# Four engines' order lists redrawn in a four-layer graph kernel

## What is computed

```python
x = layernorm(x + L0(x, adj))   # hypergraph conv, relu, layer norm, hypergraph conv, + x
x = layernorm(x + L1(x, adj))   # w = q . (adj @ k) / 16, softmax over the nodes, times v
x = layernorm(x + L2(x, adj))   # attention of 8 heads, scores * (adj + adj), softmax
x = layernorm(x + L3(x, adj))   # gated attention:
#   gate = sigmoid(deg * Wd + bd); xg = x * gate
#   QK = sigmoid(xg @ Wqk.T + bqk); s = (QK @ QK.T / 16) * adj; attn = s / (sum(s) + 1e-6)
#   out = relu(attn @ xg @ Wl.T + bl + xg @ Wr.T)
```

## Time and profile before

| | |
|---|---|
| median of 3 runs | 1077.64 us (1073.41 to 1079.28) |
| the profiled execution | 1074.29 us, span 1072.5 us |
| TensorE busy | 951.3 us (89%), mean granted clock 0.964 |
| VectorE busy | 881.4 us (82%) |
| GpSimd busy | 737.1 us (69%) |
| ScalarE busy | 711.0 us (66%) |
| HBM | 41 GB/s over the span |

### The profile page before, as it was taken

How to read it: one execution, slowest core, us unless ns; L and a number is a source line. 1 busy time by engine, 2 the same in 40 slices (tenths; PEclk the granted TensorE clock), 3 DMA queues, 4 the chain that set the end, 5 groups by cost and what they waited for, 6 DMA issues and landing times. The chain is left out here.

```text
span 1072.5 us, 32446 instructions
## 1 busy us (share of the span) xinstructions
PE 951.3 (89%) x11228; PEld 818.5 (76%) x11228; DVE 881.4 (82%) x2503; ACT 711.0 (66%) x1516; POOL 737.1 (69%) x1163
## 2 busy tenths in 40 slices
PE   3467789999999999999999999999999999998853
PEld 2346668888888888888888888888888888887642
DVE  4334668999999999999999999999999999988752
ACT  2234557776777777777777777777777777776642
POOL 3244566777778777777777887777777778875442
PEclk9588989999999999999999999999999999999996
DMA  7110222222212222222221222222222212211200
GB/s 203 30 31 2 56 58 59 64 59 64 60 50 53 63 57 66 66 66 62 59 60 52 53 57 66 57 66 66 66 57 61 61 51 53 59 49 46 53 24 20
DMA packets 110231, 61.80 MB, mean 58 GB/s; under 512 B 57072, under 2 KB 105840, under 8 KB 110192
## 3 DMA queue, kind: packets, MB, share of 16 engines
q1 hardware_dynamic: 110192, 61.30, 22.0%
HBM read 35.83 MB, written 8.39 MB: 41 GB/s over the span
## 5 line engine op out<-in xcount | busy, mean ns | idle before, releaser
L1219 POOL TENSOR_TENSOR gp<-late,bdb 128x512 f32<-128x512 f32 x32 | 40.6, 1270 | 98.0 <-ACT late L846 98.0
L460 PE MATMUL bank<-z1h,W 128*128 128x256 f16 x256 | 71.0, 277 | 2.9 <-DVE z1l L898 2.9
L462 PE MATMUL bank<-W,rFl 128*128 128x256 f16 x256 | 72.7, 284 | 0.0
L461 PE MATMUL bank<-W,rFh 128*128 128x256 f16 x256 | 72.7, 284 | 0.0
L460 PE MATMUL bank<-W,rFh 128*128 128x256 f16 x256 | 72.6, 284 | 0.0
L739 ACT ACTIVATE x<-preB,nbB,rsB 128x256 f32<-128x256 f32 x64 | 34.9, 593 | 55.1 <-POOL nbB L1214 55.1
L461 PE MATMUL bank<-z1l,W 128*128 128x256 f16 x256 | 70.7, 276 | 0.0
L462 PE MATMUL bank<-z1h,W 128*128 128x256 f16 x256 | 70.6, 276 | 0.0
L739 ACT ACTIVATE late<-preG,nbG,rsG 128x256 f32<-128x256 f32 x64 | 34.9, 592 | 52.6 <-POOL nbG L1214 52.6
L1289 POOL TENSOR_TENSOR late<-late,Smx 128x512 f32<-128x512 f32 x64 | 66.8, 1043 | 4.2 <-DVE Smx L1109 3.9
L766 ACT ACTIVATE r<-bank,b1c 128x256 f32<-128x256 f32 x128 | 53.4, 469 | 8.3 <-PE bank L462 6.2
(11 more groups left out here) (286 smaller groups left out, 4573.2 us busy)
## 6 DMA issues: line engine op xcount, KB each, us to landing
Vbd<-vst SPq DMA_DIRECT2D x128, 66.0 KB, 2.1
xin<-x SPq DMA_DIRECT2D x32, 256.0 KB, 2.7
xres<-x SPq DMA_DIRECT2D x32, 256.0 KB, 2.8
Kbd<-kst SPq DMA_DIRECT2D x128, 64.0 KB, 2.0
out<-late SPq DMA_DIRECT2D x32, 256.0 KB, 2.2
mrow<-mask SPq DMA_DIRECT2D x32, 128.0 KB, 3.2
atA<-adj_t SPq DMA_DIRECT2D x64, 32.0 KB, 2.3
aC<-adj SPq DMA_DIRECT2D x64, 32.0 KB, 2.1
```

The lines of the kernel that those rows point to most:

```text
L460: pe.matmul(o, sh, mh, start=start, stop=False, skip_group_check=True)
L461: pe.matmul(o, sh, ml, start=False, stop=False, skip_group_check=True)
L462: return pe.matmul(o, sl, mh, start=False, stop=stop, skip_group_check=True)
L1219: return pool.tensor_tensor(dst, src, b[:].rearrange("p (o d) -> p o d", o=1).broadcast_to([P, TILES, D]), ALU.add)
```

## The change

The four lists are replaced. Each has the same entries in another order: the same pieces run, with the same waits.

```diff
-ORDER_PE = [4, 2, 3, 1, 5, 3, 0, 4, 2, 5, 0, 4, 2, 1, 5, 0, 3, 2, 3, 0, 0, 1, 5, 4, 5, 1, 3, 5, 2, 3, 0, 0, 1, 2, 4]
-ORDER_ACT = [3, 0, 5, 1, 3, 5, 0, 2, 5, 0, 4, 4, 0, 4, 5, 1, 0, 3, 0, 1, 0, 0, 0, 0, 2, 4, 3, 1, 2, 5, 4, 3, 2, 4, 5]
-ORDER_DVE = [4, 0, 4, 0, 0, 0, 2, 0, 1, 0, 3, 0, 4, 0, 2, 4, 0, 4, 3, 5, 5, 2, 0, 1, 2, 1, 5, 1, 0, 4, 3, 3, 2, 2, 2, 3, 3, 1, 5, 4, 5, 4, 4, 0, 5, 5, 0, 1, 2, 3, 1, 5, 0, 5, 1, 0, 3, 2, 4]
-ORDER_POOL = [0, 0, 0, 1, 3, 1, 0, 4, 1, 1, 1, 1, 3, 5, 2, 2, 2, 3, 0, 0, 0, 4, 4, 4, 5, 4, 5, 0, 5, 0, 5, 0]
+ORDER_PE = [2, 1, 4, 3, 5, 0, 4, 2, 3, 2, 0, 5, 1, 4, 0, 2, 5, 3, 0, 0, 3, 1, 5, 4, 5, 1, 5, 3, 2, 3, 1, 0, 2, 0, 4]
+ORDER_ACT = [0, 4, 3, 1, 5, 2, 0, 5, 0, 3, 5, 4, 0, 4, 4, 5, 1, 0, 0, 0, 1, 0, 0, 0, 3, 2, 1, 3, 2, 5, 4, 3, 2, 4, 5]
+ORDER_DVE = [0, 0, 4, 0, 0, 2, 0, 2, 0, 1, 0, 4, 0, 4, 0, 4, 3, 5, 4, 0, 2, 2, 1, 5, 1, 3, 1, 0, 2, 5, 2, 3, 2, 4, 3, 3, 3, 1, 5, 0, 4, 5, 4, 5, 4, 1, 5, 2, 3, 1, 5, 5, 0, 1, 0, 3, 2, 4, 0]
+ORDER_POOL = [0, 0, 0, 1, 1, 0, 4, 3, 1, 1, 1, 1, 5, 2, 2, 3, 2, 0, 3, 0, 4, 0, 4, 4, 5, 4, 5, 5, 5, 0, 0, 0]
```

## The result

The changed kernel takes **1032.45 us** (median of 4 runs, 1028.01 to 1033.61), against 1077.59 for the kernel before in the same comparison. The ratio is 0.9579, with a 95% interval of 0.954 to 0.9618. The forecast was 1051 with a range of 1038 to 1068: the sign was right, and the gain of 45 us was under-estimated by 18.6. The executions of one kernel differ, and their mean granted clock with them: the changed kernel's have 0.962 three times and 0.969 in the one of 1028.01.

A forecast was written before the change was run, and what follows sets the result against it. TensorE was taken to set the pace, VectorE close behind. 22.7 us from 27 full steps plus 4 from the first steps made 26.7 off 1074.29, so 1047.6; with 3.35 up to the median, 1051, range 1038 to 1068.

The forecast's parts named there:

- (a): VectorE's HBl pair, moved clear of GpSimd's large instructions, costs 0.66 us instead of 1.94; not counted beyond the waits.
- (b), (c), (d): TensorE's waits for wrm (L598), HBl (M and D) and the row sums of r go, together 1.2 us a step.
- The floor of a full step: TensorE's step of 29.54 us, less 1.2 us of waits that can go, is 28.34 us.
- (e): Chain from sc1 over rFl, preF and xg takes 11.08 us against TensorE's 10.72: a new wait of 0.36 us a step.
- (f): Ql meets xl and pcol meets bias work, pushing preB and z1l about 0.6 us; counted at nothing, up to 0.3 a step.
- (g): In the first steps most of TensorE's waits for HBl go: 4 us won, bounds 1 and 7.
- (h): The last steps, without stream 0, keep layer 3's chain in the same order: no change, 2 us either way.
- A: Rival: nothing new is late and the new wait is hidden; 36.4 us won, 1041 us; chance 0.12.
- B: Rival: the gain comes back as small waits, a step of 29.3 us; 9.5 us won, 1068 us; chance 0.13.
- C: Rival: HBl's second half misses its gap, waits for xres+b2b, 1.15 us late; step 29.85, 1082 us; chance 0.06.
- D: Rival: GpSimd goes first when Ssb ends, rFl stands another 1.28 us; step 29.98, 1085.5 us; chance 0.06.

The follow-up runs named there:

- the undo: The changed kernel with VectorE's rFl put back behind mvF, as in the kernel before; 1021.9 us, ratio 0.9494 to the kernel before.

## Why the prediction was wrong, point by point

- **(a) HBl clear of GpSimd: right.** Predicted 0.66 us for the pair, measured 0.59. The margin was 0.4 us, and more in fact: VectorE and GpSimd in the changed kernel, from rvar on:

```profile
518.43 0.15 DVE L1015 SCALAR_TENSOR_TENSOR rvar<-bank,rmm 128x2 f32<-128x2 f32 x1
...
520.39 0.59 DVE L898 SCALAR_TENSOR_TENSOR HBl<-HT,be,HBh 128x128 f16<-128x128 f16 x2
```

```profile
521.37 1.27 POOL L1219 TENSOR_TENSOR xres<-xres,b2b 128x512 f32<-128x512 f32 x1
```

  HBl ends at 520.98, and xres+b2b starts 2.94 us behind rvar instead of 2.70. The remark that HBl's freedom buys 0.1 us by itself was made for a step that still waits for wrm, and doesn't carry over: the swap with y0 cost 1.4 us in every full step, 1.1 of them a wait of TensorE.
- **(b), (c), (d) The three waits go: right.** The trace after has none of them in full steps.
- **The floor of a full step: the term that failed.** I took 28.34 us, and the run with rFl moved shows 28.01 with no wait left. All gaps over 0.04 us in TensorE's timeline of one step add up to about 2.7 us before and to 1.2 in that run. I had read three of them, 1.41 us, left 0.07 of each for a hand-over and took the rest as fixed: 1.5 us would have stayed. But the gaps ahead of M and D and of the row sums are gone entirely, and so are those of 0.13 us ahead of s3 and of the xg turn, which the idle times don't count as waits. That is 0.33 us a step, 8.9 us in all.
- **(e) The new wait: right in what causes it and in size.** rFl waits for Ssb (predicted 1.35 us, median 1.45), and TensorE ends up waiting. I predicted 0.36 us a step; the undo gives 0.35. Two things were off. The wait stands at o1 alone, over ssum, and the xg turn has none: xg ends at 544.74 us and its turn starts at 544.81. And I had the chain start at sc1; giving it that start back won nothing.
- **(f) Smaller collisions: right at nothing.** Ql takes 1.11 us where it took 0.68, and TensorE doesn't wait for what follows.
- **(g) The first steps: the other term that failed.** I predicted 4 us, and 12.8 came. I priced the waits for HBl alone, at 4 of their 7.3 us. Between the first and the sixth HT 6.6 us of waits for HBl went, and with them 3.7 before the row sums of r and 2.1 for wrm, while some 4 us of smaller waits came; TensorE is idle 7.4 us less. The rest, 5.4 us, is busy time. I put nothing for what waits do to the granted clock. The page of the kernel before shows it, and I passed over it: among its 40 slices the clock's digits are 5, 8, 8, 9, 8 in the second to sixth.
- **(h) The last steps: 4.6 us lost, predicted nothing: right as far as the order goes.** Running the old lists there gave back 1.3, which can't be told from nothing, and at the same mean clock both orders take the same time within 0.6 us. The 4.6 are a clock of 0.84 in one profile against 0.90 in the other.
- **Rivals.** A (nothing new is late) came closest in number, 1041, for a wrong reason: the new wait was there. B was refuted by the step with wrm alone, where a removed wait was won in full. C did not happen, and its price for a full step was confirmed by the swap. D did not happen. In 24 of 25 steps rFl got in at the end of Ssb, ahead of the first sum of squares, which then took 1.72 us instead of 1.28; in the other it got in ahead of Ssb, which then took 1.51 instead of 1.05.
- **The sum.** Profile by profile: 26.7 us predicted. On top come 8.9 for the floor and 0.3 for (e), 1.3 since I took one step of 29.54 us for a mean that is 29.59, 8.8 for the first steps and 0.9 ahead of them; 4.6 at the end go off. That makes 42.3, and the spans differ by 42.1. That accounts for 15.4 of the 18.6 us by which the forecast missed; the other 3 lie in which executions were profiled. I had added 3.35 us, by which the profiled execution of the kernel before lay under its median; the changed kernel's lies 0.3 under its own. So part of the miss is luck: these 3 us and the 0.9 made it larger, and the 4.6 of the last steps smaller. The forecast's range had no room for it, because I had put its low end at the floor that I believed in and had given the first steps no more than 7.

## What to carry to other kernels

Where two engines share a resource, place an instruction against the other engine's list, not only in its own: a slot just behind a hand-over that both leave from, or where the other engine waits for this one, costs little or nothing. Before giving TensorE's step a floor, count every gap in its timeline, small ones too. Where the granted clock is below full speed, price the work there by it, and compare stretches of two profiles only beside their clocks: 4.6 us of this case's end were the clock and not the order. In the first steps of a pipeline, matmuls that nothing reads can be worth their time (8.3 us here, and nothing in the kernel before).

## What the runs showed of the hardware

- A large GpSimd instruction and a VectorE one with two SBUF inputs hold each other up, in both directions. rFl goes from 0.667 to 1.452 us beside Ssb, and the sum of squares behind it from 1.275 to 1.722. The Trainium skill, "SBUF — State Buffer", section "SBUF: two separate sides", has this as an exclusive lock, held for the whole instruction, between a VectorE instruction with two SBUF inputs and a GpSimd one that reads SBUF. The traces agree where VectorE waits: HBl's second half ends 0.15 us behind x2b both in the earlier trace rows and in the run with HBl ahead of y0. The delay of GpSimd is smaller than the instruction that it waits for, 0.45 us behind rFl's 0.67.
- VectorE came first at each hand-over read: HBl between xres+b2b and x2b, and rFl between Ssb and the sum of squares, or between rFl0 and Ssb, though GpSimd's next instruction followed without idle time.
- GpSimd's instructions on two columns do HBl no harm worth counting: a half takes 0.352 us at most in the changed kernel, with rsc, wcf and wch beside it. The other way round there is harm: veF, also of two columns, takes 0.46 us beside rFl instead of 0.23.
- 49 matmuls of 512 columns that nothing reads, put in front of waits, raised the mean granted clock between the first and the sixth HT from 0.85 to 0.93, and the program became 8.3 us faster. In the kernel before, whose waits come again in the steps behind them, the same 49 gained nothing that the interval can tell (ratio 0.9988, 0.9973 to 1.0004).
- The mean clock granted in the last five steps, 0.84 to 0.90 for the same lists, moved them by 4 us (114.7 against 110.7).
